# Attention block on one core: ten sets of query rows instead of nine, none across two batches, with half of two small moves issued by GpSimd

## The chip, the core and the metric

One NeuronCore of a Trainium2 chip runs the whole kernel as one program. The metric is the device time of one execution in microseconds. TensorE (PE) multiplies, VectorE (DVE), ScalarE (ACT) and GpSimd (POOL) do the rest, SyncE (SP) only issues DMAs. The engines run side by side and meet at semaphores; within one engine everything goes in the order in which the program is written.

## The reference

`x` is 4 batches of 128 channels by 1024 positions, all in float32.

```python
h = _group_norm(x, gn_w, gn_b)                       # 8 groups of 16 channels
q = jnp.einsum('oc,bcn->bon', qw, h) + qb[None, :, None]
k = jnp.einsum('oc,bcn->bon', kw, h) + kb[None, :, None]
v = jnp.einsum('oc,bcn->bon', vw, h) + vb[None, :, None]
attn = jnp.einsum('bcn,bcm->bnm', q, k) / jnp.sqrt(jnp.asarray(C, x.dtype))
attn = jax.nn.softmax(attn, axis=-1)
out = jnp.einsum('bnm,bcm->bcn', attn, v)
out = jnp.einsum('oc,bcn->bon', pw, out) + pb[None, :, None]
return x + out.reshape(B, C, H, W)
```

## The kernel before

**Steps.** The 4 x 1024 query positions are cut into 32 steps `c` of 128 rows, 8 to a batch; `b` is the batch of a step and `i` its place in the batch. In each step PE makes the scores of 128 queries against 1024 keys (`scores`, six matmuls of 512 columns into the PSUM tile S, of which two stand in turn), DVE copies them out with the row minimum (`drain_scores`, L654), ACT takes the exponential and the row sum (`exponentials`, L500), and the probabilities then have to be turned, so that keys lie on partitions, before they can be multiplied by the values. PE runs one step ahead of DVE: `scores(c)` waits only for the drain of step c-2. Query and key weights are multiplied together once at the start, and the products of value and output weights too, so a batch needs only `project_g` (h times the joint weight, held as a high and a low part, L278 to L284) and `value_tiles` (L302).

**Two ways of turning.** The first two and the last two steps are turned by PE (`transpose_probs`, L402), copied to SBUF by ACT and DVE, and used by `direct_unit` (L350). All others are turned in blocks of 32 x 32 by DVE (`transpose_blocks`, L663), and the blocks are then moved to their partitions by DMAs from the tile `blocks` to the tile `pT`, issued by SP, 16 to a set (`move_set`, L189). `moved_unit` (L375) multiplies them by the values.

**Sets.** Steps are grouped in sets, `SETS = (2, 4, 4, 4, 4, 4, 4, 4, 2)`. A set shares a PSUM accumulator, one reciprocal of the row sums (`invert_denominators`), one division (`divide`, DVE), one addition of the residual (`add_residual`, POOL) and one store. A batch has eight steps, so sets 2, 4 and 6 lie half in one batch and half in the next. Work on the values is counted in units, as many as steps: a unit of a set within a batch is 4 matmuls of 256 columns, a unit of a set that crosses is 8 matmuls of 2 x 64 columns (each matmul of full float32 shows as two records in the profile). Units are put into PE's program at fixed steps: 0 and 1 at steps 4 and 5, unit `m` from 2 on at step `m + LAG` with `LAG = 8`, and what remains behind the loop.

**The way of the reciprocals.** PE transposes the reciprocals of a set (`turn_rden`, L334), ACT copies them and issues their store to DRAM (`copy_rows`, L507 and L509), SP reads them back to all partitions (`spread_rows`, L197), and DVE's `divide` takes them. SP's queue is in order: `move_set(n)`, `spread_rows(n)`, `store_set(n - 2)`.

**The next batch.** During batch b, POOL makes the low part of the next batch's normalised input (`split_h`, L795) at i = 4, as soon as ACT has made `h` (`normalize`, L470). PE needs it in the third matmul of `project_g(b + 1, 0)` (L284) at i = 6. ACT then rounds the result (`round_g`, L480), and DVE makes its low part (`split_g`, L628), ahead of the drain of the next step.

Of the kernel before, what the change touches and what calls it, by code (L numbers as in the profile page):

```python
# [10 lines left out]
P = 128  # L11
Q = 32
# [4 lines left out]
GC = 4  # L17
VSPLIT = (3, 3, 2)

SETS = (2, 4, 4, 4, 4, 4, 4, 4, 2)  # L20

FIRST_UNIT_STEPS = (4, 5)
LAG = 8


def build(nc, x, vectors, weights, out):
# [22 lines left out]
    with ExitStack() as ctx:  # L49
# [20 lines left out]
        def columns(n):  # L70

            return slice(P * FIRST[n], P * (FIRST[n] + SETS[n]))

        def last_batch(n):
            return (FIRST[n] + SETS[n] - 1) // CH

        def crosses(n):

            return FIRST[n] // CH != last_batch(n)

        def divided_in(c):

            for n in range(LS - 2):
                last = FIRST[n] + SETS[n] - 1
                if c == (FIRST_UNIT_STEPS[last] + 3 if n == 0 else last + LAG + 1):
                    return n
            return None
# [52 lines left out]
        last_sums = [ACC[:, (LS - 1) % 2, 0:UW], ACC[:, LS % 2, 0:UW]]  # L140
# [19 lines left out]
        MOVED = 16 * NQ  # L160
# [5 lines left out]
        normed_ready, last_normed, out_ready, tail_out_ready, stored = map(sem, ("normed_ready", "last_normed", "out_ready", "tail_out_ready", "stored"))  # L166
        tp_psum = sem("tp_psum")
        pair_ready = [sem(f"pair_ready{f}") for f in range(HALVES)]

        xb_flat = xb[:, :, :].rearrange("p b n -> p (b n)")  # L170
# [5 lines left out]
        def blocks_view(n):  # L176
            return blocks[:, n % 2, 0:SETS[n] * N].rearrange("p (j t c q) -> p j t c q", j=NQ, t=KT, c=SETS[n])

# [3 lines left out]
        def _(sp):  # L182
            def move_set(n):
                sp.wait_ge(blocks_ready, FIRST[n + 1] - SETS[0])
                if n > 2:
                    sp.wait_ge(part_done, FIRST[n - 1])
                for a in range(NQ):
                    for j in range(NQ):
                        sp.dma_start(moved_view(n)[Q * j:Q * (j + 1), a].rearrange("p t n -> p (t n)"),  # L189
                                     blocks_view(n)[Q * a:Q * (a + 1), j].rearrange("p t c q -> p (t c q)"))\  # L190
                          .then_inc(moved[n % 2][a], 16)

            def spread_rows(n):
                sp.wait_ge(rows_stored[n % 2], 16 * (n // 2 + 1))
                if n > 1:
                    sp.wait_ge(out_ready, n - 1)
                sp.dma_start(rden_bc[:, n % 2, 0:P * SETS[n]], row_store[n:n + 1, 0:P * SETS[n]].to_broadcast([P, P * SETS[n]]))\  # L197
                  .then_inc(rows_spread[n % 2], 16)

            def store_set(n):  # L200
                if n < SPREAD_BY_DMA:
                    sp.wait_ge(out_ready, n + 1)
                else:
                    sp.wait_ge(tail_out_ready, 2 if n == LS else 3)
                at = P * FIRST[n]
                while at < P * (FIRST[n] + SETS[n]):
                    b, first = at // N, at % N
                    width = min(N, first + P * (FIRST[n] + SETS[n]) - at) - first
                    sp.dma_start(out[b, :, first:first + width], xb[:, b, first:first + width]).then_inc(stored, 16)
                    at += width  # L210
# [7 lines left out]
            spread_rows(0)  # L218
            move_set(1)
            spread_rows(1)  # L220
            store_set(0)
            for n in range(2, LS):
                move_set(n)
                if n < SPREAD_BY_DMA:
                    spread_rows(n)
                if n > 2:
                    store_set(n - 2)
# [3 lines left out]
            sp.wait_ge(stored, 16 * (NS + sum(crosses(n) for n in range(NS))))  # L231

        @block.tensor
        def _(pe):
            def group_deviations(b):
# [3 lines left out]
                if b > 1:  # L239
# [28 lines left out]
            def project_g(b, f):  # L268
# [60 lines left out]
            def turn_rden(n):  # L329
                pe.wait_ge(rden_ready, n + 1)  # L330
                pe.wait_ge(gvar_ready, min(FIRST[n + 1] // CH + 2, B))
                if n > 0:
                    pe.wait_ge(rows_ready, n)
                pe.transpose(A0[0:SETS[n], 0:P], rden[:, n % 2, 0:SETS[n]], ident[:, :]).then_inc(rows_psum, 1)  # L334
# [19 lines left out]
            def moved_unit(n, u):  # L354

                part, half = u // 2, u % 2
                b = FIRST[n] // CH + (half if crosses(n) else 0)
                if half == 0 or crosses(n):
                    pe.wait_ge(v_ready, VP * (b + 1))
                if half == 0:  # L360
                    if u == 0 and n > 1:
                        pe.wait_ge(normed_ready, n - 1)
                    if u == 2 and n == LS - 1:
                        pe.wait_ge(normed_ready, n)
                    for a in (2 * part, 2 * part + 1):
                        pe.wait_ge(moved[n % 2][a], MOVED * ((n + 1) // 2))
                to = last_sums[part] if n == LS - 1 else sums[n][:, UW * part:UW * (part + 1)]
                to = to.rearrange("p (a n) -> p a n", a=2)
                probs = moved_view(n)[:, 2 * part:2 * (part + 1)]
                tiles = range(PT * half, PT * (half + 1))  # L370
                if crosses(n):
# [493 lines left out]
```

## Time and profile before

| | us |
|---|---|
| median of 3 runs | 140.19 |
| lowest and highest | 140.17, 140.63 |
| the profiled execution, its time | 140.34 |
| its span from first to last instruction | 138.4 |
| PE busy | 129.9 |
| DVE busy | 99.5 |
| ACT busy | 64.9 |
| POOL busy | 26.1 |

The span is 1.9 us shorter than the time of the same execution; the rest lies around it. Busy time of PE counts overlapped matmuls once. An instruction that issues a DMA is not counted as busy; its time on the queue of its engine is shown with a q (SPq, ACTq). In the chain of waits a PE piece is a run of matmul records, back to back.

### The profile page before, as it was taken

How to read it: one execution, taken by the hardware profiler on the slowest of the kernel's cores; microseconds unless marked ns; L12 is line 12 of the kernel's file. 1: busy time of each engine (PE TensorE's matmuls, PEld its weight loads, DVE VectorE, ACT ScalarE, POOL GpSimd, SP SyncE). 2: the span in 40 equal slices, each digit the busy share in tenths (PEclk: the TensorE clock that was granted, in tenths of full speed). 3: DMA queues.
4: the chain of work that ended last, by engine and by line, in shares of the span. 5: the costliest groups of instructions: out<-in, count | busy, mean ns of one | idle time of the engine just before them, and what ended most of it. 6: DMA issues, size and time to landing. Idle time of an engine off the chain costs nothing.

```text
span 138.4 us, 2200 instructions
## 1 busy us (share of the span) xinstructions
PE 129.9 (94%) x743; PEld 112.5 (81%) x743; DVE 99.5 (72%) x172; ACT 64.9 (47%) x112; POOL 26.1 (19%) x33
## 2 busy tenths in 40 slices
PE   5999999997878999999999999999999999999990
PEld 5986888885656888999898888899988889998880
DVE  0577788989999678979687789756987798330222
ACT  4044689655556574634347735354544334412000
POOL 5053050750202033300032063000030012003000
PEclk9999999999999999999999999999999999999999
DMA  4960000002998699569781998699825998997512
GB/s 133 279 271 0 0 5 0 10 31 63 203 211 200 166 208 206 154 149 211 158 219 47 207 207 179 206 203 209 199 97 122 207 207 222 216 216 169 167 38 76
DMA packets 9566, 21.00 MB, mean 152 GB/s; under 512 B 2362, under 2 KB 4052, under 8 KB 9556
## 3 DMA queue, kind: packets, MB, share of 16 engines
q1 hardware_dynamic: 8816, 20.59, 61.2%
q10 hardware_dynamic: 740, 0.28, 0.7%
q8 instruction: 6, 0.10, 0.3%
q14 instruction: 4, 0.03, 0.1%
HBM read 4.07 MB, written 2.11 MB: 45 GB/s over the span
## 4 chain that ended last, share of the span: by engine, by line
PE 87%; DVE 8%; issue 3%; POOL 0%; DVEq 0%; POOLq 0%
PE ACC L375 36%; PE S L322 10%; PE S L323 9%; PE S L326 9%; PE S L266 5%; PE A L302 5%; DVE s_sb L654 3%; PE S L350 2%; PE ACC L350 2%; DVE blocks L663 2%; PE ACC L402 1%; PE A L402 1%; DVE g_lo L628 1%; DVE bn L579 1%; PE A L278 1%
## 5 line engine op out<-in xcount | busy, mean ns | idle before, releaser
L375 PE MATMUL ACC<-pT,v 128*128 128x128 f32 (+1 forms) x320 | 53.3, 317 | 0.0
L654 DVE TENSOR_SCALAR_CACHE_REDUCE s_sb<-S,row_term 128x1024 f32<-128x1024 f32 x32 | 41.0, 1281 | 16.4 <-PE S L326 16.0
L375 PEld LDWEIGHTS ACC<-pT,v 128*128 128x128 f32 x320 | 46.4, 191 | 3.9
L500 ACT ACTIVATE s_sb<-s_sb,rowmin 128x1024 f32<-128x1024 f32 x32 | 36.9, 1152 | 20.9 <-DVE s_sb L654 19.8
L663 DVE STREAM_TRANSPOSE blocks<-s_sb 128x1024 f32<-128x1024 f32 x28 | 34.7, 1239 | 0.0
L322 PE MATMUL S<-h_hi,g_hi 128*128 128x512 f32 x64 | 29.2, 457 | 0.3 <-issue 0.3
L323 PE MATMUL S<-h_lo,g_hi 128*128 128x512 f32 x64 | 25.1, 393 | 0.0
L326 PE MATMUL S<-h_hi,g_lo 128*128 128x512 f32 x64 | 19.9, 392 | 0.0
L808 POOL TENSOR_TENSOR xb<-rden_bc,xb 128x512 f32<-128x512 f32 (+1 forms) x7 | 8.4, 1198 | 49.8 <-DVE rden_bc L683 42.3
L326 PEld LDWEIGHTS S<-h_hi,g_lo 128*128 128x128 f32 x64 | 12.0, 188 | 2.8
L322 PEld LDWEIGHTS S<-h_hi,g_hi 128*128 128x128 f32 x64 | 12.1, 189 | 2.2 <-issue 0.4
L323 PEld LDWEIGHTS S<-h_lo,g_hi 128*128 128x128 f32 x64 | 12.1, 189 | 1.8
L492 ACT COPY v<-A 128x384 f32<-128x384 f32 (+1 forms) x12 | 5.3, 444 | 16.2 <-PE A L302 16.2
L302 PEld LDWEIGHTS A<-wpv,h 128*128 128x128 f32 x64 | 8.4, 190 | 3.7 <-issue 2.6
L302 PE MATMUL A<-wpv,h 128*128 128x129 f32 x64 | 9.5, 281 | 1.3 <-DVE g_lo L628 1.1
L795 POOL TENSOR_TENSOR h_lo<-h,h_hi 128x1024 fp32r<-128x1024 f32 x3 | 7.2, 2394 | 17.8 <-ACT h L470 17.8
L480 ACT ACTIVATE g_hi<-A,wpv 128x512 fp32r<-128x512 f32 x7 | 4.8, 689 | 9.5 <-PE A L284 9.5
L266 PE MATMUL S<-ident 128*128 128x128 f32 x38 | 7.5, 351 | 1.6 <-POOL ident L812 1.6
L579 DVE BATCH_NORM_STATS2 bn<-x_sb 128x6 f32<-128x512 f32 x8 | 5.3, 684 | 3.5 <-DMA x_sb<-x 3.5
L266 PEld LDWEIGHTS S<-ident 128*128 128x128 f32 x38 | 6.5, 255 | 1.6 <-POOL ident L812 1.6
L786 POOL TENSOR_TENSOR rstd<-gvar,minus_half 128x1 f32<-128x1 f32 x4 | 2.2, 553 | 29.3 <-DVE gvar L601 29.3
L465 ACT ACTIVATE h_hi<-x_sb,gshift,gscale 128x1024 fp32r<-128x1024 f32 (+1 forms) x5 | 5.2, 1067 | 2.3 <-DVE gshift L612 1.8
(90 smaller groups left out, 102.9 us busy)
## 6 DMA issues: line engine op xcount, KB each, us to landing
pT<-blocks SPq DMA_DIRECT2D x112, 128.0 KB, 2.5
rden_bc<-row_store SPq DMA_DIRECT2D x6, 256.0 KB, 3.4
x_sb<-x SPq DMA_DIRECT2D x1, 1024.0 KB, 6.3
out<-xb SPq DMA_DIRECT2D x8, 128.0 KB, 2.8
out<-xb SPq DMA_DIRECT2D x4, 256.0 KB, 2.9
x_sb<-x SPq DMA_DIRECT2D x2, 256.0 KB, 3.0
x_sb<-x SPq DMA_DIRECT2D x1, 512.0 KB, 4.1
w_in<-weights ACTq DMA_DIRECT2D x2, 128.0 KB, 3.5
```

The source lines that it names most:

```text
L266: pe.matmul(S[:, 0, BANK:BANK + P], ident[:, :], ident[:, :], start=True, stop=True)
L302: last = pe.matmul(A1[:, PW1 * u:PW1 * (u + 1)], h[:, P * t:P * (t + 1)], wpv[:, 0:PW1], start=True, stop=True)
L322: pe.matmul(S[:, c % 2, ks], g_hi[:, qs], h_hi[:, b % 2, ks], start=True, stop=False)
L323: pe.matmul(S[:, c % 2, ks], g_hi[:, qs], h_lo[:, b % 2, ks], start=False, stop=False)
L326: last = pe.matmul(S[:, c % 2, ks], g_lo[:, qs], h_hi[:, b % 2, ks], start=False, stop=True)
L375: last = pe.matmul(to, v[:, b % 3, t, :], probs[:, :, t, :], start=(t == 0), stop=(t == KT - 1))
L500: act.activation(s_sb[:, c % 3, :], s_sb[:, c % 3, :], ACT.Exp, bias=rowmin[:, c % CH:c % CH + 1], scale=-1.0, accum_out=den[:, n % 2, k:k ...
L579: dve.bn_stats(bn[:, f, :], x_sb[:, b, BANK * f:BANK * (f + 1)]).then_inc(bn_ready, 1)
L654: dve.tensor_scalar(s_sb[:, c % 3, :], S[:, c % 2, :], row_term[:, b % 2, i:i + 1], None, ALU.add, ALU.min, accum_out=rowmin[:, i:i + 1]). ...
L663: dve.transpose(blocks_view(n)[:, :, :, k, :].rearrange("p j t q -> p t j q"), s_sb[:, c % 3, :].rearrange("p (t j q) -> p t j q", t=KT, j ...
L795: pool.tensor_tensor(h_lo[:, b % 2, :], h[:, :], h_hi[:, b % 2, :].bitcast(F32), ALU.subtract).then_inc(h_lo_ready, 1)
L808: pool.tensor_tensor(xs, rden_bc[:, n % 2, 0:P * SETS[n]], xs, ALU.add).then_inc(out_ready, 1)
```

## The change

1. `SETS` becomes `(2, 2, 4, 4, 4, 4, 4, 4, 2, 2)`: sets 1 and 8 have two steps, sets 2 to 7 have four, and none lies in two batches. The code for sets that cross goes. Unit `u` of a small moved set takes half of the key tiles and all 256 columns, so all units are 4 matmuls of 256 columns.
2. Units 0 to 3 stand at steps 5, 7, 9, 10, and `LAG` becomes 7, so unit 4 stands at step 11. Sets 0 and 1 are divided at steps 9 and 12.
3. Sets 1 and 8 are moved by 16 DMAs of half the size: SP issues eight (`move_set`), POOL the other eight (`move_half`). On POOL `move_half(1)` stands at step 4, ahead of `split_h(1)`, and `move_half(8)` at step 30, ahead of `add_residual(6)`.
4. `spread_rows` goes from SP to ACT, a step behind the store of the same rows. SP stores a set one move later (`store_set(n - 3)`). The transposes of the reciprocals of sets 0 and 1 go to the PSUM tile A1, and `project_g(1, 0)` waits until ACT has copied them.
5. At the end the last moved set has two steps and one accumulator instead of four and two. PE does the direct units first, then units 28 and 29; the last store is of 256 columns instead of 512.

```diff
-SETS = (2, 4, 4, 4, 4, 4, 4, 4, 2)
-FIRST_UNIT_STEPS = (4, 5)
-LAG = 8
+SETS = (2, 2, 4, 4, 4, 4, 4, 4, 2, 2)
+FIRST_UNIT_STEPS = (5, 7, 9, 10)
+FIRST_DIVIDED_STEPS = (9, 12)
+LAG = 7
...
+        def pieces(n):
+            return NQ if SETS[n] == GC else NQ // 2
...
                 for a in range(NQ):
-                    for j in range(NQ):
-                        sp.dma_start(moved_view(n)[Q * j:Q * (j + 1), a].rearrange("p t n -> p (t n)"),
...
+                    for j in range(pieces(n)):
+                        sp.dma_start(moved_piece(n, a, j), blocks_piece(n, a, j)).then_inc(moved[n % 2][a], 16)
...
+                    if b == 1 and f == 0:
+                        pe.wait_ge(rows_ready, 2)
                 pe.wait_ge(h_hi_ready, HALVES * b + f + 1)
...
-                if crosses(n):
-                    cs = slice(2 * Q * half, 2 * Q * (half + 1))
-                    to, probs, tiles = to[:, :, cs], probs[:, :, :, cs], range(KT)
...
-                if c >= LAG + SETS[0]:
+                if c >= LAG + GC:
                     value_unit(c - LAG)
...
+            def spread_rows(n):
+                act.wait_ge(rows_stored[n % 2], 16 * (n // 2 + 1))
+                if n > 1:
+                    act.wait_ge(out_ready, n - 1)
+                act.dma_start(rden_bc[:, n % 2, 0:P * SETS[n]], row_store[n:n + 1, 0:P * SETS[n]].to_broadcast([P, P * SETS[n]]))\
+                   .then_inc(rows_spread[n % 2], 16)
...
+            def move_half(n):
+                pool.wait_ge(blocks_ready, FIRST[n + 1] - SETS[0])
+                if n > 2:
+                    pool.wait_ge(part_done, FIRST[n - 1])
+                for a in range(NQ):
+                    for j in range(pieces(n), NQ):
+                        pool.dma_start(moved_piece(n, a, j), blocks_piece(n, a, j)).then_inc(half_moved[n][a], 16)
...
+                if c in (FIRST[2], DIRECT):
+                    move_half(FIRST.index(c) - 1)
                 if i == 4 and b < L:
                     split_h(b + 1)
```

POOL's program around step 4. The names: `xb` is the residual with bias, `h_lo` the low part of batch 1, which `project_g(1, 0)` needs. Before:

```order
L802 TENSOR_SCALAR xb<-x_sb,out_bias 128x1024 [waits x1_loaded]
L795 TENSOR_TENSOR h_lo<-h,h_hi 128x1024 [waits h_hi_ready,h_ready]
L802 TENSOR_SCALAR xb<-x_sb,out_bias 128x1024 [waits xs_loaded] x2
L808 TENSOR_TENSOR xb<-rden_bc,xb 128x256 [waits xb_ready,normed_ready]
L786 TENSOR_TENSOR rstd<-gvar,minus_half 128x1 [waits h_hi_ready,h_ready,gvar_ready]
```

The same place in the change:

```order
L798 TENSOR_SCALAR xb<-x_sb,out_bias 128x1024 [waits x1_loaded]
L812 DMA pT<-blocks 32x512 [waits blocks_ready]
L812 DMA pT<-blocks 32x512 x7
L791 TENSOR_TENSOR h_lo<-h,h_hi 128x1024 [waits h_hi_ready,h_ready]
L798 TENSOR_SCALAR xb<-x_sb,out_bias 128x1024 [waits xs_loaded] x2
L804 TENSOR_TENSOR xb<-rden_bc,xb 128x256 [waits xb_ready,normed_ready]
L782 TENSOR_TENSOR rstd<-gvar,minus_half 128x1 [waits h_hi_ready,h_ready,gvar_ready]
```

Eight DMA issues and a wait for the blocks of step 3 now stand ahead of `h_lo`.

PE's program from the end of `scores(5)` on. Before (L278 to L284 are `project_g(1, 0)`, L350 is unit 1, L334 the transpose of set 1's reciprocals, L302 `value_tiles(1, 0)`):

```order
L326 MATMUL S<-h_hi,g_lo 128x512 x2
L350 MATMUL ACC<-pair_T,v 128x256 x4
L322 MATMUL S<-h_hi,g_hi 128x512
...
L326 MATMUL S<-h_hi,g_lo 128x512 x2
L278 MATMUL A1<-h_hi,wa_hi 128x512
L279 MATMUL A1<-h_hi,wa_lo 128x512
L284 MATMUL A1<-h_lo,wa_hi 128x512
...
L326 MATMUL S<-h_hi,g_lo 128x512 x2
L334 MATMUL A0<-ident,rden 4x128
L302 MATMUL A1<-wpv,h 128x129 x3
```

In the change (L345 is unit 0 and, after step 7, unit 1):

```order
L316 MATMUL S<-h_hi,g_lo 128x512 x2
L329 MATMUL A1<-ident,rden 2x128
L345 MATMUL ACC<-pair_T,v 128x256 x4
L312 MATMUL S<-h_hi,g_hi 128x512
...
L316 MATMUL S<-h_hi,g_lo 128x512 x2
L268 MATMUL A1<-h_hi,wa_hi 128x512
L269 MATMUL A1<-h_hi,wa_lo 128x512
L274 MATMUL A1<-h_lo,wa_hi 128x512
...
L316 MATMUL S<-h_hi,g_lo 128x512 x2
L292 MATMUL A1<-wpv,h 128x129 x3
L345 MATMUL ACC<-pair_T,v 128x256 x4
```

The third matmul of `project_g(1, 0)` still stands between `scores(6)` and `scores(7)`; unit 0 stands a step later, unit 1 two steps later.

## Rows read from the trace of the kernel before

**Rows 1.** The page: busy time; then 40 slices of the span, in tenths.
```profile
PE 129.9 (94%) x743; PEld 112.5 (81%) x743; DVE 99.5 (72%) x172; ACT 64.9 (47%) x112; POOL 26.1 (19%) x33
...
PE   5999999997878999999999999999999999999990
...
DVE  0577788989999678979687789756987798330222
...
PEclk9999999999999999999999999999999999999999
```
**Rows 2.** The chain of waits: start us, length us, what. Steps 10 to 13.
```profile
43.66 1.73 PE ACC L375 x8
45.38 0.23 PE S L322
...
53.08 1.73 PE ACC L375 x8
```
**Rows 3.** The chain of waits again: units of sets that cross, and the end.
```profile
56.88 1.78 PE ACC L375 x16
...
64.79 1.89 PE ACC L375 x16
...
117.74 3.57 PE ACC L375 x32
...
122.19 1.79 PE ACC L375 x16
123.98 0.66 PE S L340 x6
...
131.54 3.47 PE ACC L375 x16
135.03 0.43 DVE rden_bc L696
135.49 0.42 DVE xb L701
```
**Rows 4.** Timeline of DVE, steps 4 to 10: start us, us, instruction, idle before.
```profile
25.39 1.24 DVE L663 STREAM_TRANSPOSE blocks<-s_sb 128x1024 f32<-128x1024 f32 x1
...
29.85 1.28 DVE L654 TENSOR_SCALAR_CACHE_REDUCE s_sb<-S,row_term 128x1024 f32<-128x1024 f32 x1 [0.67 <-PE S L326]
...
32.28 0.72 DVE L628 SCALAR_TENSOR_TENSOR g_lo<-A,wpv,g_hi 128x512 fp32r<-128x512 f32 x1
...
38.30 1.24 DVE L663 STREAM_TRANSPOSE blocks<-s_sb 128x1024 f32<-128x1024 f32 x1
```
**Rows 5.** Timeline of PE, steps 6 to 10.
```profile
30.11 0.39 PE L284 MATMUL A<-h_lo,wa_hi 128*128 128x512 f32 x1
...
42.97 0.68 PE L302 MATMUL A<-wpv,h 128*128 128x129 f32 x4 [0.69 <-DVE g_lo L628]
```
**Rows 6.** Timeline of ACT, step 6: rounding of the next g.
```profile
30.55 0.69 ACT L480 ACTIVATE g_hi<-A,wpv 128x512 fp32r<-128x512 f32 x1 [1.25 <-PE A L284]
```
**Rows 7.** Timeline of POOL, step 4.
```profile
25.10 2.39 POOL L795 TENSOR_TENSOR h_lo<-h,h_hi 128x1024 fp32r<-128x1024 f32 x1 [4.86 <-ACT h L470]
```
**Rows 8.** Groups by line and form: the same shape on POOL and on DVE.
```profile
L808 POOL TENSOR_TENSOR xb<-rden_bc,xb 128x512 f32<-128x512 f32 x6 | 7.6, 1274 | 42.3 <-DVE rden_bc L683 42.3
...
L683 DVE TENSOR_TENSOR rden_bc<-ACC,rden_bc 128x512 f32<-128x512 f32 x6 | 4.0, 667 | 1.1 <-PE ACC L375 1.1
```
**Rows 9.** DMA issues by line: duration ns min/median/max; then issue to landing of L189.
```profile
L509 ACTq DMA_DIRECT2D row_store<-rden_rows x7: 247/247/507, 25.2 to 107.1; - x7
...
L189 SPq DMA_DIRECT2D pT<-blocks x112: 507/592/1477, 32.3 to 125.7; - x112
...
DMA to landing us min/median/max: 2.2/2.5/3.5
```
**Rows 10.** Windows: PE, PEld, DVE, ACT, POOL busy; clock, DMA share, GB/s.
```profile
40.00:42.00 2.00, 2.00 (x11) 1.54 (x10) 2.00 (x3) 1.29 (x2) 0.00 (x0) 1.00 0.96 209
```

More of the change, by code:

```diff
@@ L70, in columns, with divided_step, landed @@
         def columns(n):
[L72 to L79, printed above, removed]
-        def divided_in(c):
[L83 to L87, printed above, removed]
+            b, i = FIRST[n] // CH, FIRST[n] % CH
+            return b, slice(P * i, P * (i + SETS[n]))
+        def divided_step(n):
+            return FIRST_DIVIDED_STEPS[n] if n < 2 else FIRST[n] + SETS[n] + LAG
+        def divided_in(c):
+            return next((n for n in range(SPREAD_BY_DMA) if divided_step(n) == c), None)
+        def pieces(n):
+            return NQ if SETS[n] == GC else NQ // 2
+        def landed(n):
+            return sum(16 * pieces(k) for k in range(1, n + 1) if k % 2 == n % 2 and k < LS)
         w_in = sb("w_in", [P, 4, P])
@@ L159, in build @@
         moved = [[sem(f"moved{k}_{a}") for a in range(NQ)] for k in range(2)]
-        MOVED = 16 * NQ
+        half_moved = {n: [sem(f"half_moved{n}_{a}") for a in range(NQ)] for n in (1, LS - 1)}
         part_done = sem("part_done")
@@ L203, in store_set @@
                 else:
[L204 to L210, printed above, removed]
+                    sp.wait_ge(tail_out_ready, 1 if n == LS else 2)
+                b, cs = columns(n)
+                sp.dma_start(out[b, :, cs], xb[:, b, cs]).then_inc(stored, 16)
             for f in range(HALVES):
@@ L230, in _ @@
             store_set(LS - 1)
-            sp.wait_ge(stored, 16 * (NS + sum(crosses(n) for n in range(NS))))
+            sp.wait_ge(stored, 16 * NS)
         @block.tensor
@@ L354, in moved_unit @@
             def moved_unit(n, u):
-                part, half = u // 2, u % 2
-                b = FIRST[n] // CH + (half if crosses(n) else 0)
-                if half == 0 or crosses(n):
+                b, size = FIRST[n] // CH, SETS[n]
+                a0, width, half = (2 * (u // 2), 2, u % 2) if size == GC else (0, NQ, u)
+                if u == 0:
                     pe.wait_ge(v_ready, VP * (b + 1))
-                if half == 0:
[L361 to L370, printed above, removed]
-                if crosses(n):
-                    cs = slice(2 * Q * half, 2 * Q * (half + 1))
-                    to, probs, tiles = to[:, :, cs], probs[:, :, :, cs], range(KT)
-                for t in tiles:
-                    last = pe.matmul(to, v[:, b % 3, t, :], probs[:, :, t, :], start=(t == 0), stop=(t == KT - 1))
+                    if n > 1:
+                        pe.wait_ge(normed_ready, n - 1)
+                    else:
+                        for f in range(HALVES):
+                            pe.wait_ge(pair_ready[f], 2)
+                if half == 0:
+                    for a in range(a0, a0 + width):
+                        pe.wait_ge(moved[n % 2][a], landed(n))
+                        if n in half_moved:
+                            pe.wait_ge(half_moved[n][a], 16 * (NQ - pieces(n)))
+                to = sums[n].rearrange("p (a n) -> p a n", a=NQ)[:, a0:a0 + width]
+                for t in range(PT * half, PT * (half + 1)):
+                    last = pe.matmul(to, v[:, b % 3, t, :], moved_view(n)[:, a0:a0 + width, t, :], start=(t == 0), stop=(t == KT - 1))
                 last.then_inc(part_done, 1)
@@ L430, in _ @@
                     value_tiles(b, 2)
-                if c - 1 in FIRST[1:LS]:
-                    turn_rden(FIRST.index(c - 1) - 1)
+                if i == 3 and (b == 0 or c > CH):
+                    turn_rden(2 * b if b > 0 else 0)
+                if i == 5:
+                    turn_rden(2 * b + 1)
                 if i == 6 and b < L:
@@ L442, in _ @@
                     value_unit(FIRST_UNIT_STEPS.index(c))
-                if c >= LAG + SETS[0]:
+                if c >= LAG + GC:
                     value_unit(c - LAG)
-            value_unit(STEPS - LAG)
-            transpose_probs(STEPS - 1)
-            for m in range(STEPS - LAG + 1, FIRST[LS - 1]):
+            for m in range(STEPS - LAG, FIRST[LS - 1]):
+                if m == FIRST[LS - 1] - 1:
+                    transpose_probs(STEPS - 1)
                 value_unit(m)
@@ L672, in divide @@
             def divide(n):
[L673 removed]
+                dve.wait_ge(part_done, {LS: DIRECT, LS - 1: STEPS}.get(n, FIRST[n] + SETS[n]))
                 if n < SPREAD_BY_DMA:
@@ L841, in _ @@
                     add_residual(divided_in(c))
-            add_residual(SPREAD_BY_DMA - 1)
+            for n in range(SPREAD_BY_DMA):
+                if divided_step(n) >= STEPS:
+                    add_residual(n)
 def kernel(x, L0_conv_gn_w, L0_conv_gn_b, L0_conv_qw, L0_conv_qb, L0_conv_kw, L0_conv_kb,
```

101 lines of the change are left out of this document (46 added, 55 removed).

## The prediction

> **What bounds the kernel now.** I read the page first [rows 1]: PE is busy 94% of the span, its clock is granted in full in every slice, and the only slices in which it falls below nine tenths after the start are the tenth to the thirteenth, at some 31 to 45 us. There DVE is at nine tenths. Then the chain of waits: from 43.66 us on it is PE without a gap, scores and units in turn [rows 2], up to the last unit at 131.54 + 3.47, behind which come two DVE instructions and a store [rows 3]. So there are two stages. Up to about step 10 DVE sets the pace, with PE waiting at points such as 0.69 us before the value tiles [rows 5]. From step 11 on PE does, and every microsecond of PE work taken out there is a microsecond of time. Third, the few rows around step 6, since two engines and a half meet there [rows 4 to 7].
>
> **PE work that goes.** (a) The sets that cross have 12 units. A unit of the other kind takes 1.73 us in the chain [rows 2]; the twelve take 21.63 in all (7.35 for set 2, 7.14 each for sets 4 and 6; the first is 1.78, the dearest 1.89, the last 3.57 for two and 1.79 [rows 3]). 21.63 - 12 x 1.73 = 0.87. They lie in the stage that PE bounds: **-0.85 us**.
> (b) The last broadcast is of 4 columns instead of 6, at 0.66 / 6 = 0.11 us each [rows 3]: **-0.2**. The last store is half as large, of which I take **-0.1**.
> (c) With LAG 7 and units at steps 9 and 10, four units instead of three are done by the end of step 10 (before: 0, 1, 2). One unit of 1.73 leaves the stage that PE bounds for the one that DVE bounds. It doesn't all vanish. At step 9 `project_g(1, 1)` waits for DVE as before, then unit 2 follows, so `scores(10)` ends 1.73 later, and the value tiles start not at 42.97 after a wait of 0.69 [rows 5] but at about 43.85, when PE is free; they take 0.45 in turn, unit 3 takes 1.73, and `scores(11)` starts at 46.05 instead of 45.38 [rows 2]. That is 0.65 later with 1.73 less to do: **-1.1**.
> Units 0 and 1, moved to steps 5 and 7, lie where DVE has the longer step (1.28 + 1.24 us and its extras), and I cost them at 0.1 or less; the transpose of set 1's reciprocals, which now holds unit 0 until DVE has inverted at about 26.8, makes `scores(6)` end at 30.0 where its drain began at 29.85 [rows 4].
> Sum of these: -2.25.
>
> **Moves with a shorter lead.** Unit n's data now have three steps instead of four. Set 2's blocks are ready when DVE ends at 38.30 + 1.24 less the overlap, 39.4 [rows 4]; its first unit stands after `scores(11)`, at about 47.4. It needs 8 of the 16 pieces: the eighth is issued 7 x 0.59 to 0.63 later, at 43.8, and lands 2.5 later [rows 9], at 46.3. Spare: 1.1 us. For the later sets the spare is between 0.6 and 2. But ACT now reads the reciprocals back while a move is on (sets 2, 4, 6 at steps 13, 21, 29), not behind it. The 16 engines are at 0.96 of their time at 209 GB/s during a move [rows 10], so 256 KB more take 1.2 us from it, and three of the units can be late by 0 to 0.6. I take **+0.25** in all, bounds 0 and 1.5. ACT's own wait for the stored rows stands a step, about 3 us, behind the store, and its exponential has as much idle time as it needs; 0, and its issue times (0.25 each for the store [rows 9]) lie in idle time too.
> Without the next part the sum is -2.0: 138.3 against 140.34.
>
> **POOL's eight issues.** POOL's program now has eight DMA issues ahead of `h_lo`, and they wait for the blocks of step 3, which DVE finishes at 25.39 + 1.24 = 26.63 [rows 4]. Before, `h_lo` ran from 25.10 to 27.49 [rows 7]. Now it ends at 26.63 + X + 2.39 + 0.1 = 29.1 + X, where X is what eight issues take on POOL; it is an engine in order, and `h_lo` needs it whole. Who waits: L284, which before ran at 30.11 [rows 5], then ACT's rounding, 0.44 later, 0.69 long [rows 6], then `g_lo` on DVE, ready to start at about 32.3 [rows 4]. Counting back, L284 may start at 31.2 without delaying DVE. So X may be 31.2 - 29.1 = 2.1 us, 0.26 an issue. All beyond that is a stall of PE and DVE together (`scores(7)` stands behind L284, the drain of step 7 behind `g_lo`), at a place that DVE bounds, and nothing in the fixed order can be done meanwhile. It is paid in full: X - 2.1.
> The trace has no DMA issue on POOL. Bounds: ACT's cheapest, 0.247, of 2 KB [rows 9], gives X = 2.0 and no stall; SP's dearest, 1.477 [rows 9], gives 11.8 and a stall of 9.7. The nearest row is SP's own for the same transfers, 0.592 in the median: X = 4.7, stall 2.6. But POOL takes 1.27 us where DVE takes 0.67 for the same shape [rows 8], 1.9 times; an issue that POOL has to work out itself may be dearer by as much, 1.13. I take the middle, 0.86 an issue: X = 6.9, stall **+4.8**. The Trainium skill ("DMA: Bandwidth & Descriptors", section "Latency and other measured facts") gives about 1 us to the first byte on the GpSimd path, which it calls the emission overhead, against about 0.6 us for the hardware path. The second agrees with SP's 0.592 in this trace; no row shows the first. With 1 us taken as the time of an issue, an estimate from that page, X would be 8, the stall 5.9 and the time 144.2.
> The same halves for set 8, at step 30, cost nothing by this account: they start at about 114, end at 121, and land by 124, ahead of unit 28 at about 129.5; the residual of set 6 behind them on POOL is then 5 us late, but ACT's copy that waits for it is needed at 129.5 too.
>
> **Sum.** -2.25 + 0.25 + 4.8 = +2.8, on 140.34: 143.1. The median of the runs is 0.15 below the profiled execution: **143.0 us**.
>
> **Rivals.**
> 1. *POOL issues as cheaply as ACT* (0.25 to 0.4). Then `h_lo` is in time or at most 1.1 us late, and the PE terms stand: 138.2 to 139.3. For it: ACT's rows; that POOL has nothing else to do. Against: SP's rows are more than twice ACT's for just these transfers. Chance 0.26. It decides at X = 4.1, where the stall eats the 2.0, that is at 0.51 us an issue.
> 2. *In between*, 0.42 to 0.6 an issue, X of 3.4 to 4.8: 139.5 to 140.9, within 0.5%. Chance 0.14.
> 3. *The moved data come late*: the shorter lead costs the full 1.5 and recurs at each of the six sets; with cheap issues 139.6 (138.1 + 1.5). It needs landings of 3.5 us, the longest seen [rows 9], at every first piece group. Chance 0.03, inside the other cases; it adds no case of its own sign.
> 4. *DVE takes the freed time*: if from step 11 on DVE were the bound, the 0.85 of (a) and the 1.1 of (c) would not come. DVE has 2.5 us of drain and transpose in a step of 3.1 and is busy 72% [rows 1], so I give it no more than 0.02, at 141 without a stall.
> The forecast, an expensive issue on POOL, has 0.58; it spans 141.0 (0.6 an issue) to 146 (1.2).
>
> **How the numbers follow.** A measurement of this kernel can tell about 0.5%, 0.7 us. Slower by more: the forecast's 0.58 and a little of rival 4, 0.6. Within: 0.14. Faster: 0.26. As cases of both signs hold much of the chance, the range reaches over both: 138.2 to 146.0; the forecast's own is 141.0 to 146.0. Left out are the dearest issues (SP's 1.477 each would give 147.9), 0.08, and something under 138.2, 0.07.
>
> **What would show it.** Right: in the changed trace `h_lo` for batch 1 starts at 33 to 35 us instead of 25.1, POOL's queue shows eight issues of 0.7 to 1 us from 26.6 on, PE idles before its third projection matmul for 3 to 5 us and the page has a hole in PE and DVE near slice 9 or 10. From step 11 on all units show 1.73, and the tail from the last unit to the end is as before. Wrong: `h_lo` done by 31; or issues of 0.25. If L366's first units of sets 2, 3, 5 or 7 wait for a DMA, the lead is the cause. If ACT waits at L507 for the stored rows, the queue change costs something that I put at nothing.

## The result: slower by 6.7%, through a wait at the end that the prediction did not have

The changed kernel takes 149.8 us in the median of 4 runs (148.87 to 150.39) against 140.36 before: 1.0665 times as long, 95% interval 1.0602 to 1.0728. The forecast was 143.0 with a range up to 146.0. Slower came true, the size did not, and more than half of the loss lies where the forecast saw none. In all runs below an execution more than 1.5% above the fastest of its kernel counts as slow and is left out of the ratio.

The page of the changed kernel answers to [rows 1] (busy time, then 40 slices of a span of 148.4 us):

```profile
PE 133.2 (90%) x646; PEld 112.5 (76%) x646; DVE 99.4 (67%) x172; ACT 64.9 (44%) x113; POOL 34.9 (24%) x50
...
PE   5999997729989999999999999999999998079991
...
DVE  0588789862997788799779787966886792001122
...
PEclk9999999995999999999999999999999999956999
```

Two holes are new in PE's row, in the ninth slice and in slices 34 to 36, and in the tenth slice and in slices 36 and 37 the granted clock stands at about half. The waits of PE by length (engine line <- what it waited for: us in all, times, longest) name both:

```profile
PE ACC L366 <- DMA pT<-blocks: 5.0, 1, 5.0
...
PE A L274 <- POOL h_lo L791: 2.9, 1, 2.9
```

**The early hole.** POOL's timeline, and PE's behind it:

```profile
27.00 4.14 POOL L812 DMA_DIRECT2D pT<-blocks  x8 [6.71 <-DVE blocks L667]
31.16 2.36 POOL L791 TENSOR_TENSOR h_lo<-h,h_hi 128x1024 fp32r<-128x1024 f32 x1
```
```profile
33.57 0.79 PE L274 MATMUL A<-h_lo,wa_hi 128*128 128x512 f32 x1 [2.86 <-POOL h_lo L791]
```

Eight issues take 4.14 us on POOL, 0.52 each. `h_lo` (the low part of the next batch's input) starts at 31.16 instead of 25.10 [rows 7], and the third projection matmul at 33.57 instead of 30.11 [rows 5].

**The late hole.** PE's timeline at the end of the changed kernel (L366 are units of moved sets, L393 the transposes of the last step, L345 further on the direct units):

```profile
122.05 3.62 PE L366 MATMUL ACC<-pT,v 128*128 128x256 f32 x16
130.64 3.75 PE L366 MATMUL ACC<-pT,v 128*128 128x256 f32 x8 [4.97 <-DMA pT<-blocks]
134.19 1.90 PE L393 MATMUL A<-ident,s_sb 128*128 128x128 f32 x8
135.90 1.92 PE L366 MATMUL ACC<-pT,v 128*128 128x256 f32 x8
```

Units 24 and 25 need the first half of set 7's pieces, unit 26 the second. It waits 4.97 us, and then takes 3.75 us where a unit takes 1.73 [rows 2]. The data are late because they take long to land: these are the times from issue to landing of the pieces that SP issues in three stretches, 114.3 to 119.5, 119.4 to 122 and 122 to 124.6 us ([rows 9] had 2.5 in the median and 3.5 at most):

```profile
DMA to landing us min/median/max: 2.4/2.5/4.2
...
DMA to landing us min/median/max: 2.5/4.4/5.4
...
DMA to landing us min/median/max: 5.3/5.7/6.3
```

Windows over the same time, in the columns of [rows 10]; the seventh figure behind the length is the DMA engines' share:

```profile
120.00:122.00 2.00, 2.00 (x14) 1.70 (x13) 1.97 (x4) 1.02 (x3) 0.98 (x2) 1.00 0.85 186
122.00:124.00 2.00, 2.00 (x12) 1.77 (x11) 1.29 (x4) 1.64 (x3) 2.00 (x5) 1.00 1.04 254
124.00:126.00 2.00, 1.67 (x8) 1.14 (x6) 0.15 (x1) 0.00 (x0) 1.98 (x4) 1.00 1.07 221
126.00:128.00 2.00, 0.00 (x0) 0.00 (x0) 0.00 (x0) 0.00 (x0) 0.33 (x1) 1.00 1.04 236
128.00:130.00 2.00, 0.00 (x0) 0.00 (x0) 0.00 (x0) 0.00 (x0) 0.00 (x0) 0.78 0.95 246
130.00:132.00 2.00, 1.36 (x3) 1.18 (x4) 0.00 (x0) 0.00 (x0) 0.00 (x0) 0.50 0.57 148
132.00:134.00 2.00, 2.00 (x6) 1.58 (x5) 0.00 (x0) 0.00 (x0) 0.00 (x0) 0.50 0.41 96
```

POOL's second eight pieces begin at 121.02, and from 122 to 128 the DMA engines are busy all the time (a share of 1.04 to 1.07), at 221 to 254 GB/s. PE is idle for 5 us, and its granted clock falls to the lower of its two levels, 1.2 GHz, at about 129, and stays there until about 136.

**Where the 10.0 us of span are.** I read off PE's timeline when the last two matmuls of the scores of a step start, in each kernel's profiled execution, and when the last unit ends (us):

| | step 7 | step 8 | step 11 | step 31 | last unit ends |
|---|---|---|---|---|---|
| before | 31.27 | 34.81 | 46.13 | 116.25 | 135.01 |
| changed | 35.87 | 40.16 | 50.79 | 120.72 | 145.2 |
| e1, POOL's issues behind h_lo | 31.75 | 36.93 | 47.52 | 118.08 | 142.1 |
| e3, direct units first | 35.90 | 40.21 | 50.84 | 121.20 | 139.2 |
| e5, both | 31.51 | 36.71 | 47.29 | 117.39 | 134.8 |
| e6, both and units moved up | 31.44 | 34.01 | 45.91 | 115.79 | 133.6 |

By step 11 the changed kernel is 4.66 us behind; in the twenty steps to 31 it makes up 0.19; from there to the last unit it takes 24.5 us instead of 18.8, 5.7 more, though it has a unit less to do (eight against nine). What follows the last unit is 0.2 shorter. 4.66 - 0.19 + 5.7 - 0.2 = 10.0.

### The profile page after: what moved, and what is told of

Same layout as the page of the kernel before. It is cut to its first block, busy times and chain, and to the rows that moved or that the text cites. A ratio compares the mean times of both kernels' runs of the same rounds, so it can differ in the third digit from the quotient of the medians.

```text
span 148.4 us, 2045 instructions
## 1 busy us (share of the span) xinstructions
PE 133.2 (90%) x646; PEld 112.5 (76%) x646; DVE 99.4 (67%) x172; ACT 64.9 (44%) x113; POOL 34.9 (24%) x50
## 4 chain that ended last, share of the span: by engine, by line
PE 75%; SPq 6%; POOL 4%; DVE 4%; DMA 4%; issue 4%; POOLq 0%; DVEq 0%
PE ACC L366 29%; PE S L312 9%; PE S L316 8%; PE S L313 8%; SPq L195 6%; PE A L292 5%; PE S L254 5%; DMA pT<-blocks 4%; POOL pT L812 2%; DVE blocks L667 2%; PE S L345 2%; POOL h_lo L791 2%; PE A L274 1%; PE ACC L345 1%; PE A L393 1%
## 5 line engine op out<-in xcount | busy, mean ns | idle before, releaser
L366 PE MATMUL ACC<-pT,v 128*128 128x256 f32 x224 | 54.9, 391 | 5.0 <-DMA pT<-blocks 5.0
L366 PEld LDWEIGHTS ACC<-pT,v 128*128 128x128 f32 x224 | 42.3, 196 | 11.9 <-issue 5.9
L312 PE MATMUL S<-h_hi,g_hi 128*128 128x512 f32 x64 | 30.7, 480 | 0.3 <-issue 0.3
L313 PE MATMUL S<-h_lo,g_hi 128*128 128x512 f32 x64 | 25.6, 400 | 0.0
L804 POOL TENSOR_TENSOR xb<-rden_bc,xb 128x512 f32<-128x512 f32 (+1 forms) x8 | 9.1, 1134 | 51.3 <-DVE rden_bc L687 42.9
L812 POOL DMA_DIRECT2D pT<-blocks x16 | 8.2, 517 | 18.1 <-DVE blocks L667 18.1
L292 PEld LDWEIGHTS A<-wpv,h 128*128 128x128 f32 x64 | 9.0, 195 | 1.7 <-DVE g_lo L630 0.4
L702 DVE COPY pair_T<-A 128x512 f32<-128x512 f32 x2 | 1.4, 690 | 12.0 <-PE A L393 12.0
```

The costliest lines, as they stand in the source:

```text
L292: last = pe.matmul(A1[:, PW1 * u:PW1 * (u + 1)], h[:, P * t:P * (t + 1)], wpv[:, 0:PW1], start=True, stop=True)
L312: pe.matmul(S[:, c % 2, ks], g_hi[:, qs], h_hi[:, b % 2, ks], start=True, stop=False)
L313: pe.matmul(S[:, c % 2, ks], g_hi[:, qs], h_lo[:, b % 2, ks], start=False, stop=False)
L366: last = pe.matmul(to, v[:, b % 3, t, :], moved_view(n)[:, a0:a0 + width, t, :], start=(t == 0), stop=(t == KT - 1))
L804: pool.tensor_tensor(xb[:, b, cs], rden_bc[:, n % 2, 0:P * SETS[n]], xb[:, b, cs], ALU.add).then_inc(out_ready, 1)
L812: pool.dma_start(moved_piece(n, a, j), blocks_piece(n, a, j)).then_inc(half_moved[n][a], 16)
```

## The experiments

Each was timed against the kernel before on the same chip. The ratios are those to the kernel before, which took 140.36 to 140.59 us in the median of the four groups of runs; times of different groups compare within some 0.2 us.

### e1: POOL's issues behind h_lo

```diff
-                if c in (FIRST[2], DIRECT):
-                    move_half(FIRST.index(c) - 1)
                 if i == 4 and b < L:
                     split_h(b + 1)
+                if c in (FIRST[2], DIRECT):
+                    move_half(FIRST.index(c) - 1)
```

> The changed kernel with one step moved: on POOL the eight issues of set 1's half (move_half(1)) stand behind split_h(1) instead of ahead of it. Theory A (the issues hold h_lo, PE idles 2.86 us before the third projection matmul, and its clock is then halved from 33.6 to 37 us, which costs 1.8 more): h_lo runs at 25.1 to 27.5 again, both terms go, and the time falls by 4.5 to 4.7 us, from 149.8 to about 145.2. Rival B (the early stage is bound by DVE anyway, and the wait only shows what would be lost elsewhere): the wait goes but less than 1 us of time. Rival C (the clock falls in this stretch for another reason): the wait goes, the granted clock at 33 to 37 us stays near 0.57, and the time falls by 2.9 only.

Measured: 147.07 us, ratio 1.0448 (1.0396 to 1.0499). 2.7 us less, not 4.6. The early wait and the half clock are gone, so C falls, and the gain is far over B's 1 us. But at step 11 e1 is still 1.4 us behind the kernel before (47.52 against 46.13). It takes 5.2 us from step 7 to step 8, where the kernel before takes 3.5. PE's timeline there:

```profile
30.59 0.39 PE L274 MATMUL A<-h_lo,wa_hi 128*128 128x512 f32 x1
...
33.55 0.91 PE L292 MATMUL A<-wpv,h 128*128 128x129 f32 x6 [1.17 <-DVE g_lo L630]
34.29 1.89 PE L345 MATMUL ACC<-pair_T,v 128*128 128x256 f32 x8
```

PE idles 1.17 us, does the value tiles, and only then unit 1, which now lies between DVE and the scores it needs for step 8. A (both terms go in full) was too much. By step 11 3.3 us are gained, and behind the stall a second fault is left, which e6 tests.

### e2: POOL holds set 8 back until set 7 has landed

```diff
                     pool.wait_ge(part_done, FIRST[n - 1])
+                    for a in range(NQ):
+                        pool.wait_ge(moved[(n - 1) % 2][a], landed(n - 1))
```

> The changed kernel with one wait added: before its eight issues for set 8, POOL waits until all pieces of set 7 have landed. Theory A (set 7's last pieces land late, 5.7 us instead of 2.5, because POOL's pieces share the DMA engines with them): they land in 2.5 to 3 us, unit 26 waits about 1.3 us (its last piece is issued at 124.2 and it is wanted at 125.7) instead of 5.0, PE's clock does not fall, and the time drops by 6 to 6.5 us, to about 143.5. Rival B (ACT's read-back of 256 KB at 119.7 and SP's own store are what delays them): landing stays near 5 us, the wait near 5 us, the time at 149 to 150. Rival C (the lead alone is too short): the wait is 1.3 us whatever the landing was, same number as A, told apart by the landing times.

Measured: 146.01 us, ratio 1.0388 (1.0345 to 1.0431). Landing of the pieces issued from 121 to 123.8, then the unit that waits for them:

```profile
DMA to landing us min/median/max: 3.6/3.8/4.0
```
```profile
126.96 3.23 PE L366 MATMUL ACC<-pT,v 128*128 128x256 f32 x8 [2.38 <-DMA pT<-blocks]
```

POOL's pieces are worth 1.9 us of landing (5.7 to 3.8) and 2.6 of the wait. The wait of 2.38 is still followed by the half clock, which A did not expect, so 3.8 us came instead of 6.3. From step 31 to the last unit it takes 20.9 us, 3.5 less than the changed kernel. B and C are both part of the rest; e9 parts them.

This run also has an exception. Up to POOL's issues of set 8 its program is that of the changed kernel, and PE idles before `h_lo` as there, but in the profiled execution the clock stays full behind it. The third projection matmul, and the window 33 to 37 us:

```profile
33.76 0.50 PE L274 MATMUL A<-h_lo,wa_hi 128*128 128x512 f32 x1 [2.88 <-POOL h_lo L791]
```
```profile
33.00:37.00 4.00, 2.95 (x15) 2.32 (x16) 1.98 (x4) 1.95 (x4) 2.90 (x3) 1.00 0.25 64
```

The changed kernel has 0.57 in that window. So the same idle stretch was not followed by the half clock every time, and some 1 us of the gain of this one execution (145.50; the others took 145.87 to 146.47) comes from there.

### e9: POOL's half of set 8 and ACT's read-back held back until set 7 has landed

```diff
-                if i == 7:
+                if i == 7 and b < L:
                     spread_rows(2 * b + 1)
...
+            for a in range(NQ):
+                act.wait_ge(moved[1][a], landed(LS - 2))
+            spread_rows(LS - 2)
             copy_pair(STEPS - 1)
```

with the wait of e2 on POOL.

> The changed kernel where, at the end, neither POOL's half of set 8 nor ACT's read-back of set 7's reciprocals is issued until set 7's pieces have landed. Set 7's last pieces are then alone on the DMA engines but for SP's own. With POOL alone held back they landed in 3.8 us (5.7 in the changed kernel) and unit 26 waited 2.4 us (5.0). Theory (the two queues share the blame for what is over 2.5): landing 2.5 to 2.8 us, unit 26 waits 1.0 to 1.4, which is what the lead alone costs (last piece issued about 10 us after the first, wanted 11.3 us after it), the clock does not fall, and the time is near 149.8 - 3.8 - 2.8 = 143.2. Rival (the pieces slow one another, SP's queue having built up by then): landing stays at 3.8 and the time at 146.

Measured: 143.91 us, ratio 1.0245 (1.0168 to 1.0323). Landing in the same stretch (121 to 124), and unit 26:

```profile
DMA to landing us min/median/max: 2.4/2.7/4.1
```
```profile
128.06 1.97 PE L366 MATMUL ACC<-pT,v 128*128 128x256 f32 x8 [1.50 <-DMA pT<-blocks]
```

Close to the theory, which had 1.0 to 1.4 us of wait and 143.2 us. The wait of 5.0 is made of 2.6 from POOL's half of set 8, 0.9 from ACT's read-back, and 1.5 that the lead alone is too short. These shares are for the order in which the causes were taken away; the read-back alone was not held back in any run. From step 31 to the last unit it takes 18.4 us, 6.0 less than the changed kernel. After 1.50 us the clock stayed full (a run of 8 matmuls shows 1.97).

### e3: direct units ahead of unit 26

```diff
-            for m in range(STEPS - LAG, FIRST[LS - 1]):
-                if m == FIRST[LS - 1] - 1:
-                    transpose_probs(STEPS - 1)
-                value_unit(m)
+            value_unit(STEPS - LAG)
+            transpose_probs(STEPS - 1)
             broadcast_rden(LS - 1)
             broadcast_rden(LS)
             value_unit(DIRECT)
             value_unit(DIRECT + 1)
+            for m in range(STEPS - LAG + 1, FIRST[LS - 1]):
+                value_unit(m)
...
-                dve.wait_ge(part_done, {LS: DIRECT, LS - 1: STEPS}.get(n, FIRST[n] + SETS[n]))
+                dve.wait_ge(part_done, {LS: DIRECT, LS - 1: STEPS, LS - 2: DIRECT}.get(n, FIRST[n] + SETS[n]))
```

The last pair of lines makes DVE's division of set 7 wait for 30 units instead of 28, since two direct units now come ahead of its last.

> The changed kernel with PE's end in another order: behind unit 25 come the transposes of the last step, the broadcasts and the two direct units (4.8 us of work that needs no moved data), and only then units 26 to 29. The DMAs are issued as before. If the cost at the end is only that unit 26 is wanted before its data are there, whatever delays them, the wait of 5.0 us falls under 0.5 and the clock stays full: 149.8 - 5.0 - 2.8 = 142 us. If the halved clock has another cause than the idle stretch, it stays low for some 5 us and the time is near 145.

Measured: 143.88 us, ratio 1.0233 (1.0168 to 1.0297). The DMAs land as late as before (5.9 us in the median for the last), and PE hardly notices:

```profile
132.05 7.14 PE L366 MATMUL ACC<-pT,v 128*128 128x256 f32 x32 [0.51 <-DMA pT<-blocks]
```

From step 31 to the last unit it takes 18.0 us, 6.5 less than the changed kernel. 5.9 us of the time came back, not 7.8: the profiled execution is 0.5 behind at step 31, with a wait of 0.37 for a DMA on the way, and 0.9 us of waits remain at the end.

### e4 and e7: idle matmuls in the two waits

```diff
+                    if b == 1 and f == 0:
+                        for _ in range(12):
+                            pe.matmul(ACC[:, 1, 0:P], ident[:, :], ident[:, :], start=True, stop=True)
                     pe.wait_ge(h_lo_ready, b)
```

> The changed kernel with 12 idle matmuls (identity times identity, 128 columns, 2.7 us at the full clock) put ahead of the wait for h_lo in the first projection of batch 1; nothing else moves. Theory A (the clock is halved because PE idled before h_lo): the granted clock is full at 33 to 37 us, PE still starts the third projection matmul at 33.6, and the time falls by 1.6 to 1.9 us, to 148.0. Rival B (the clock has nothing to do with the idle time): clock still halved, time unchanged or longer by the dummies' rest.

e7, in the changed kernel, ahead of unit 26:

```diff
+                if m == FIRST[LS - 1] - 2:
+                    pe.wait_ge(rowmin_ready, STEPS - 1)
+                    for _ in range(22):
+                        pe.matmul(S[:, 0, BANK:BANK + P], ident[:, :], ident[:, :], start=True, stop=True)
```

> The changed kernel with 22 idle matmuls (128 columns, 4.9 us at the full clock) ahead of unit 26, nothing else. They fill the wait for set 7's last pieces. If the halved clock behind that wait is due to the idle stretch, unit 26 takes 1.73 us instead of 3.75 and the transposes 0.87 instead of 1.69, and the time falls by 2.8 us to 147.0; the data still come at the same time. If the clock falls for another reason, it stays near 149.8.

Measured, e4: 147.22, 150.27, 150.64 and 150.72 us. The lowest lies alone, 2% below the others, so there is no ratio, and a gain in time is not shown. But in the profiled execution (150.72) the clock is what the expectation says. The window 33 to 37 us, of the changed kernel and then of e4:

```profile
33.00:37.00 4.00, 3.43 (x9) 2.76 (x10) 0.79 (x2) 1.81 (x3) 2.71 (x3) 0.57 0.14 40
```
```profile
33.00:37.00 4.00, 3.53 (x22) 2.73 (x21) 1.89 (x3) 1.81 (x3) 3.16 (x3) 1.00 0.25 66
```

With the idle time filled the clock is full. At step 8 e4 stands at 39.58 after a start 0.45 later, so 1.0 us was gained of the 1.8 that slow matmuls cost. I put the rest down to DVE, which has part of this stretch; no run tests that. In the profiled execution it is lost again at unit 16, which waits for a move:

```profile
94.89 1.97 PE L369 MATMUL ACC<-pT,v 128*128 128x256 f32 x8 [1.25 <-DMA pT<-blocks]
```

There the pieces, issued from 86.5 to 91 us, took 3.9 us in the median. ACT's read-back had gone out at 85.47, with the first piece of the set, at 85.32.

e7: 148.91 us, ratio 1.0588 (1.0529 to 1.0646). Its end:

```profile
125.67 5.08 PE L442 MATMUL S<-ident 128*128 128x128 f32 x44
130.59 1.97 PE L366 MATMUL ACC<-pT,v 128*128 128x256 f32 x8
132.39 1.04 PE L393 MATMUL A<-ident,s_sb 128*128 128x128 f32 x8
```

The data come at the same time, and unit 26 and the transposes run at full clock. From step 31 to the last unit this takes 21.6 us, 2.9 less than in the changed kernel, where 2.8 were expected. The profiled execution took 147.46, but the median gained only 0.9, with executions between 147.46 and 149.28. The clock term is shown in the trace; its worth in the median is not, and why the other executions are longer stays open. In the two kernels with idle matmuls the filled stretch kept the full clock both times; e2 shows that an unfilled one can keep it too.

### e5: both orders

The edits of e1 and e3.

> Both order changes at once: POOL's issues for set 1 behind split_h(1), and PE's direct units ahead of unit 26. Theory (two separate faults, no others of size): their gains add. The first alone gave 147.1, the second alone 143.9, against 149.8: 149.8 - 2.7 - 5.9 = 141.2 us, clock full. Rival (what is repaired early turns up as a wait for moved data later, since the DMAs keep their own pace): a wait for a DMA of 1 us or more at unit 16 or unit 26, and 142.5 or more.

Measured: 140.36 us in 10 runs (139.43 to 141.11), ratio 0.9992 (0.9966 to 1.0018). No wait for a DMA shows in its trace, and the clock is full. The two reorderings, which move no byte and drop no work, take back 9.4 us. That is more than the sum of the parts, 8.6. In the profiled executions the surplus is 1.3 us of span (10.4 against 3.1 and 6.0), and it is as large as short waits that e1 and e3 have and e5 has not: 0.4 us for moved data in e1 besides the long one, 0.9 in e3. Why they are gone in e5 is not shown.

### e6: units 0 and 1 moved up

```diff
-FIRST_UNIT_STEPS = (5, 7, 9, 10)
+FIRST_UNIT_STEPS = (5, 6, 9, 10)
...
                 scores(c)
+                if c in FIRST_UNIT_STEPS and c < CH:
+                    value_unit(FIRST_UNIT_STEPS.index(c))
...
-                if c in FIRST_UNIT_STEPS:
+                if c in FIRST_UNIT_STEPS and c >= CH:
                     value_unit(FIRST_UNIT_STEPS.index(c))
```

on top of e5.

> As the run with both orders, and PE's units 0 and 1 stand right behind scores(5) and scores(6), ahead of the transpose of set 1's reciprocals and of the projection. Theory (unit 0 held behind the transpose, and unit 1 behind the value tiles, cost 0.4 and 1.2 us in the early stage: PE idled 1.8 us ahead of the transpose and the drain of step 8 came late): scores(8) ends 1 to 1.5 us earlier, 140 us. Rival (DVE bounds these steps whatever PE does): less than 0.4 us.

Measured: **138.65 us** (138.03 to 139.58), ratio **0.9882** (0.9837 to 0.9926): 1.2% less than the kernel before, and less than the changed kernel. PE's timeline, in which unit 0 fills the time before the transpose, and unit 1 that before the projection:

```profile
24.64 1.89 PE L345 MATMUL ACC<-pair_T,v 128*128 128x256 f32 x8
26.60 0.27 PE L329 MATMUL A<-ident,rden 128*2 128x128 f32 x1
...
28.09 1.89 PE L345 MATMUL ACC<-pair_T,v 128*128 128x256 f32 x8
29.63 0.58 PE L268 MATMUL A<-h_hi,wa_hi 128*128 128x512 f32 x1
```

At step 11 it stands at 45.91, before the 46.13 of the kernel before, with one unit more behind it, and 1.4 us before e5 (47.29). So the rival, less than 0.4 us, falls.

### e8: the read-back later

```diff
-            return FIRST_DIVIDED_STEPS[n] if n < 2 else FIRST[n] + SETS[n] + LAG
+            return FIRST_DIVIDED_STEPS[n] if n < 2 else FIRST[n] + SETS[n] + LAG + 1
...
-                if i == 5:
+                if i == (5 if b == 0 else 7):
                     spread_rows(2 * b)
-                if i == 7:
-                    spread_rows(2 * b + 1)
+                if c == 7 or (i == 0 and b > 1):
+                    spread_rows(1 if c == 7 else 2 * b - 1)
...
                 exponentials(c)
+            spread_rows(2 * B - 1)
```

on top of e6. The last line is the read-back of set 7, behind the loop.

> As the unit_fill run, with ACT reading the reciprocals back two steps later for the even sets and one later for the odd ones, and the divisions one step later, so that 256 KB no longer go beside the first half of a move. Theory (ACT's read-back at the start of a move delays its pieces, 2.5 to 3.6 us and more, and unit 16 then waits up to 1.2 us): the pieces of sets 3, 5 and 7 that come first land in 2.4 to 2.6 us, PE no longer waits for a DMA at the units 8 and 16, and the time is 0.3 to 1 us below the unit_fill run. Rival (the landing times are late enough to be harmless on average): no difference beyond 0.3 us, or a later wait of DVE for the rows.

Measured: ratio 0.993 (0.9901 to 0.996) against e6's 0.9882 (0.9837 to 0.9926). Seven of ten executions took 138.84 to 140.37 us, 139.48 in the median; three took 141.94 to 142.30. So it is no faster than e6 (138.65), and by the medians 0.8 us slower, with intervals that overlap. The gain in the middle did not come, as e6 had no such wait left there to lose: both reach step 31 at the same time (115.75 and 115.79). At the end the last two read-backs, at 114.68 and 117.79, now meet set 7's second half, whose last pieces take 7.0 to 9.1 us to land. The trace is of an execution of 142.18 us, and unit 26 shows

```profile
128.40 8.83 PE L366 MATMUL ACC<-pT,v 128*128 128x256 f32 x32 [2.31 <-DMA pT<-blocks]
```

Four units in 8.83 us instead of 7.14: the half clock again, behind an idle stretch of 2.3 us. The seven shorter executions have a mean granted clock of 0.998 to 1.000 over the whole span, so no such fall shows in them.

### e10 and e11: SP alone

In e10 all pieces of set 8, in e11 all pieces of set 1 are issued by SP, on top of e6.

```diff
-            return NQ if SETS[n] == GC else NQ // 2
+            return NQ if SETS[n] == GC or n == LS - 1 else NQ // 2
...
-                if c in (FIRST[2], DIRECT):
+                if c == FIRST[2]:
                     move_half(FIRST.index(c) - 1)
```

That is e10. In e11 the conditions are `n == 1` and `c == DIRECT`.

> As the unit_fill run (138.65), with all 16 pieces of set 8 issued by SP and none by POOL. SP comes to them after the 16 pieces of set 7 and a store, at about 121.3, and at 0.59 us each needs until 130.7; the last lands at 133.2, and unit 28 is wanted at 129.9. Theory (the split over two queues is worth its place for set 8): PE waits 3 us before unit 28, its clock halves, time 142 to 144. Rival (the queue only saves issue time, the bytes are the limit): within 0.5 us of 138.65.

> As the unit_fill run (138.65), with all 16 pieces of set 1 issued by SP and none by POOL. They are issued from 26.6 to 36.1 and land by 38.7; unit 2 stands at about 39. Theory (POOL's share of set 1 buys nothing, since nobody waits for it): 138.65 within 0.4 us. Rival (the last piece comes just late for unit 2): a wait of 0.5 to 1 us there, 139.2 to 139.6.

Measured, e10: 143.93 us in the median of four (142.49 to 144.78), ratio 1.018 (1.0069 to 1.029). SP's issues of set 8 last from 120.90 to 131.79, and units 28 and 29 show

```profile
133.35 5.38 PE L366 MATMUL ACC<-pT,v 128*128 128x256 f32 x16 [3.42 <-DMA pT<-blocks]
```

The last piece is issued at 131.2 and lands by 133.3. So POOL's half of set 8 has its use, once the order of PE's work leaves it time. e11: ratio 0.9857 (0.9751 to 0.9962), the same as e6 within the interval. It rests on two executions, 138.01 and 139.17; the other two took 142.32 and 144.07. In the profiled one, 142.32, PE's work from 6 to 14 us takes about twice as long as in e6 (a weight load 0.55 us instead of 0.30), though the record has the granted clock at 1.00 there; why is open. POOL's half of set 1 buys nothing that two executions can show.

## Why the prediction was wrong, and where it was right

- **"Slower" came true by luck.** The forecast had it from one term, the stall of 4.8 by expensive issues on POOL. The prediction named its own point of balance, 0.51 us an issue, where the stall eats the gain of 2.0. An issue took 0.52. By its own sum that gives 138.2 + 2.0 = 140.2 us, no change, which was its rival 2 at a chance of 0.14. Even with the 2.7 us that e1 gave back for this order, half clock included, the sum is 140.9, within 0.5% of the kernel before. What made the kernel 9.4 us slower is in terms that the sum put at nothing or next to it: the wait at the end, the half clock behind both idle stretches, and the place of units 0 and 1.
- **The bound, and the PE work that goes (-2.25): the bound right, the size only in part shown.** e6 has the same work as the changed kernel and takes 138.65 where the sum without the stall gave 138.2 for the median. But e6 has another order; e5, which leaves units 0 and 1 where the prediction had them, takes 140.36. Term (a), the twelve crossing units, is smaller in the trace than put: nine of them lie between steps 11 and 31 and cost 0.70 more than nine others, but the changed kernel takes only 0.19 less there. One more transpose of reciprocals (0.11) stands against it; the rest I cannot account for.
- **Units 0 and 1 at no more than 0.1: wrong.** They cost about 1.7 (e5 140.36, e6 138.65). The step that failed was "lie where DVE has the longer step": the steps are long for DVE, but the idle time of PE lies ahead of the transpose and the projection, and the units stood behind it.
- **POOL's eight issues, +4.8: the mechanism right, the term mis-sized in two ways.** `h_lo` waited as told. An issue takes 0.52, not 0.86, so SP's 0.592 was the better row and the factor between POOL and DVE for arithmetic said nothing on issues. PE's idle time was 2.86, against a stall of 4.8. What was missing is the half clock behind it, 1.8 us of slower matmuls, of which e4 got 1.0 back by step 8. Together the order cost 3.3 us at step 11 (50.79 against 47.52 in e1).
- The page that I weighed there, the Trainium skill's "DMA: Bandwidth & Descriptors" ("Latency and other measured facts"), has about 1 us to the first byte for a DMA issued from GpSimd. It was read as the time of an issue; the trace has 0.52 for that, and from issue to landing 2.6 in the median for POOL's eight pieces of set 1, against 2.5 for SP's pieces in [rows 9]. The prediction also said that the page's 0.6 us to the first byte on the hardware path agrees with SP's 0.592. That compares two things: 0.592 is how long the issue takes on SP's queue, and no row shows a first byte.
- **"The same halves for set 8 cost nothing": the step that failed worst.** I asked when POOL's own pieces would land, not what they would do to the pieces already on the way. They and ACT's read-back took the landing of set 7's last pieces from 2.7 us (e9) to 5.7. I also had POOL start at about 114. It began at 121.02, when the blocks of step 29 were ready, beside the second half of set 7, the one that unit 26 waits for.
- **"Moves with a shorter lead", +0.25 with a bound of 1.5: wrong at its place.** I worked out the lead of a set's first half only, at a place inside the loop. Behind step 31 there are no scores between the units, so unit 26 follows unit 25 at once: the lead of the second half was 11.3 us (114.4 to 125.7). In e9, with the same lead (115.3 to 126.6), the last piece is issued 10.1 us after the first, 0.67 an issue where I had 0.59 to 0.63, and with a landing of 2.5 to 2.7 that makes 12.6 to 12.8: 1.3 to 1.5 us more than the lead, the wait of 1.5 in e9. Rival 3 named late data, but with 1.5 us spread over six sets, not 5.0 at one, and with no clock behind it.
- Of the signs that the prediction named for being right, the hole near slice 9 was there. The others were smaller than named: `h_lo` started at 31.2 (33 to 35 forecast), issues took 0.5 us (0.7 to 1 forecast), PE idled 2.86 us (3 to 5 forecast). The signs of a short lead, waits at the first units of sets 2, 3, 5 or 7, were absent: only unit 26, the third of set 7, waited. "The tail from the last unit to the end is as before" held; the hole lay ahead of the last units.

So, for the end: 5.0 of wait, 2.0 and 0.8 of half clock, less 1.73 for a unit, 0.2 for the broadcast and some 0.2 for crossing units, makes the 5.7 of the table.

## What to carry to other kernels

When a lag is shortened, check the lead of every consumer, and most of all of those behind the loop, where the work that had stood between them ends. Before an idle queue is given transfers, look at what its engine does next and what is already in flight: here a second queue saved issue time (e10), and its transfers made those of the first queue land later (e2). Where two engines set the pace in turn, work moved into an idle stretch has to stand in front of the wait, not behind it: that order alone was worth 1.7 us here.

## What the runs showed of the hardware

- DMA issues on POOL take 0.50 us each in the median (eight in 4.14), about as long as SP's 0.592 for pieces of twice the size, and POOL does nothing else meanwhile.
- With idle stretches of 2.3 (e8), 2.4 (e2), 2.9 (four traces), 3.4 (e10), 4.6 (e4), 4.8 (e1) and 5.0 us PE's granted clock fell to half, during them or behind them, for about 3.4 us with those up to 3.4 and about 6.8 us with those from 4.6 on. One stretch of 2.88 us, in e2, was not followed by it. After 1.5 us (e9) and 1.8 us (the changed kernel, ahead of the transpose at 26.79) it stayed full, as in the whole kernel before, whose longest stretch was 1.57, at the start. Idle matmuls kept it full both times they were tried.
- A transfer of 128 KB between two SBUF tiles lands in 2.5 us in the median while SP's queue alone feeds the engines at some 210 GB/s. It took 5.7 with POOL's pieces and ACT's read-back beside it (up to 254 GB/s), 3.8 with POOL's held back (e2) and 2.7 with both held back (e9).
